# Waiting separately for the up and the down weights of the mixed slots, and a constant distance of three slots for the row requests

## The reference

```python
x = x + _L0_attn_ref(_layernorm(x, axis=-1), ...)     # delta-rule attention, 8 heads
x = x + _L0_ffn_ref(_layernorm(x, axis=-1), ...)      # mixture of experts
```

```python
cw = _combine_weights(xt, gate_w)          # four of 16 experts for each token
for e in range(E):
    a = _swiglu(xt @ expert_up_w[e].T)     # silu(gate half) * up half, 352 wide each
    out = out + cw[:, e:e + 1] * (a @ expert_down_w[e].T)
out = out + _swiglu(xt @ shared_up_w.T) @ shared_down_w.T
```

## Time and profile before

| what | value |
|---|---|
| median of three runs | 1292.75 us |
| profiled execution, its own time | 1290.94 us |
| its span, first to last instruction | 1289.1 us |
| PE busy | 1227.8 us, 95% of the span |
| DVE busy | 844.3 us, 65% |
| ACT busy | 367.2 us, 28% |
| POOL busy | 339.4 us, 26% |
| mean granted clock of TensorE | 0.977 |

### The profile page before, as it was taken

One profiled execution on the slowest core, in us unless ns is written; L12 is line 12 of the kernel. 1 busy time (PEld: TensorE's weight loads), 2 busy tenths in 40 slices (PEclk: granted clock), 3 DMA queues, 4 the chain that ended last, 5 costly groups with the idle time before them and its releaser, 6 DMA issues. The chain is left out here.

```text
span 1289.1 us, 26529 instructions
## 1 busy us (share of the span) xinstructions
PE 1227.8 (95%) x8747; PEld 750.4 (58%) x8747; DVE 844.3 (65%) x2352; ACT 367.2 (28%) x808; POOL 339.4 (26%) x401
## 2 busy tenths in 40 slices
PE   7979999999999999999999989999999999998985
PEld 6857778877776555444444544555555555554543
DVE  4897698768769475244511475777777777775763
ACT  4755655654453323220000011111111111111111
POOL 1302324322333122114653021222221122122212
PEclk9989999998997999999999998999999999998998
DMA  5434853742653494275457784878787878787642
GB/s 166 92 52 86 146 122 82 163 126 62 133 123 125 123 240 106 89 242 195 178 185 252 215 200 109 226 177 224 171 225 186 213 175 214 182 220 186 151 93 25
DMA packets 214306, 202.42 MB, mean 157 GB/s; under 512 B 72608, under 2 KB 154528, under 8 KB 214176
## 3 DMA queue, kind: packets, MB, share of 16 engines
q1 hardware_dynamic: 130080, 112.25, 33.3%
q10 hardware_dynamic: 67456, 54.24, 16.2%
q0 software_dynamic: 16640, 34.24, 12.2%
HBM read 123.76 MB, written 81.08 MB: 159 GB/s over the span
## 5 line engine op out<-in xcount | busy, mean ns | idle before, releaser
L2321 DVE STREAM_TRANSPOSE ups<-a 32x96 f32<-32x96 f32 (+1 forms) x1136 | 296.9, 261 | 35.4
L2191 POOL DMA_INDIRECT out<-front_region,ix x64 | 99.7, 1558 | 375.7 <-DMA out<-front_region,ix 148.5
L2446 PE MATMUL pD<-w,ups 128*128 (+1 forms) x384 | 176.7, 596 | 1.0 <-DVE ups L2321 0.7
L2433 PE MATMUL pG<-w,xsT 128*128 x512 | 162.9, 461 | 0.4 <-ACT g L2260 0.3
L2433 PE MATMUL pU<-w,xsT 128*128 x512 | 161.9, 459 | 0.0
L981 PE MATMUL pProj<-front_region 128*128 128x256 f32 x624 | 155.7, 393 | 2.2 <-ACT front_region L716 1.6
L2433 PEld LDWEIGHTS pG<-w,xsT 128*128 128x128 f32 x512 | 96.1, 189 | 75.2 <-issue 34.1
L2433 PEld LDWEIGHTS pU<-w,xsT 128*128 128x128 f32 x512 | 97.3, 190 | 54.2
L981 PEld LDWEIGHTS pProj<-front_region 128*128 128x128 f32 x624 | 113.8, 192 | 20.4 <-ACT front_region L716 2.1
L2260 ACT ACTIVATE g<-pG 128x352 f32<-128x352 f32 x72 | 33.4, 464 | 314.5 <-issue 121.6
L2446 PEld LDWEIGHTS pD<-w,ups 128*128 128x128 f32 (+1 forms) x384 | 71.9, 190 | 79.8 <-issue 69.2
(11 more groups left out here) (312 smaller groups left out, 1795.7 us busy)
## 6 DMA issues: line engine op xcount, KB each, us to landing
w<-in_expert_T SPq DMA_DIRECT2D x80, 384.0 KB
front_region<-in_expert_T ACTq DMA_DIRECT2D x64, 352.0 KB, 4.3
slot_rows<-zeros SPq DMA_DIRECT2D x72, 266.0 KB
front_region<-slot_rows ACTq DMA_DIRECT2D x288, 64.0 KB, 3.8
front_region<-in_expert_T ACTq DMA_DIRECT2D x32, 256.0 KB, 3.5
front_region<-in_L_attn_hidden_states SPq DMA_DIRECT2D x16, 256.0 KB, 4.0
x2r<-in_L_attn_hidden_states SPq DMA_DIRECT2D x16, 256.0 KB, 4.1
partial_sums<-x2r SPq DMA_DIRECT2D x16, 256.0 KB, 3.1
```

The lines of the kernel that those rows point to most:

```text
L2191: pool.indirect_dma_start(out=flat, out_offset=bass.IndirectOffsetOnAxis(ap=to[:, 0:1], axis=0), in_=y[(q - 1) % RING][:, :], in_offset=No ...
L2321: dve.transpose(aT[par][B * to:B * to + B, 0:n, rows], a[rows, 0:len(IC) * P].rearrange("p (c n) -> p c n", c=len(IC))[:, 0:n, B * to:B * ...
L2433: mm = pe.matmul(out[:, 0:I], rows[:, k, :], w[:, bass.ds(weights[0], 1), 2 * I * k + at:2 * I * k + at + I], start=(k == 0), stop=(k == D ...
L2446: return pe.matmul(out[:, :], gated_[0:m, c, :], w[0:m, bass.ds(weights[0], 1), at:at + D], start=(c == 0), stop=(c == 2))
```

## The change

Two independent edits, both in the slot stage.

1. The 14 pieces of a mixed slot now count on two semaphores: the eight of up weights on `s_wm`, the six of down weights on `s_wmd`. The gate product of a mixed slot waits for the up weights only. A new wait for the down weights stands ahead of the down product of the mixed slot, which is in the next body.
2. The helper `rows_by` is gone. Body 0 asks for rows 0 to 3, and body q from 1 on asks for rows q+3. Requests for routing data stay two slots ahead. The wait inside `load_rows` is the same expression, so it now looks for a transpose one slot earlier.

```diff
-                for r in range(max(2, rows_by(q - 1)), rows_by(q)):
-                    load_rows(r)
+                    load_rows(2)
+                if q + RING - 1 < NQ:
+                    load_rows(q + RING - 1)
...
-                    act.dma_start(wm[0:n, h, at:at + width], rows[0:n, at:at + width]).then_inc(s_wm, 16)
+                    act.dma_start(wm[0:n, h, at:at + width], rows[0:n, at:at + width]).then_inc(s_wm if c < DC else s_wmd, 16)
...
-                        pe.wait_ge(s_wm, 32 * (DC + len(IC)) * (before_mixed(q) + 1))
+                        pe.wait_ge(s_wm, 32 * DC * (before_mixed(q) + 1))
...
+                    if is_mixed(q - 1):
+                        pe.wait_ge(s_wmd, 32 * len(IC) * (before_mixed(q - 1) + 1))
```

More of the change, by code:

```diff
@@ L2091, in experts @@
     s_pos, s_read, s_routed = sem("pos_ready"), sem("counts_read"), sem("routed")
-    s_wm, s_out = sem("mixed_weights_loaded"), sem("mixed_rows_out")
+    s_wm, s_wmd, s_out = sem("mixed_up_loaded"), sem("mixed_down_loaded"), sem("mixed_rows_out")
     route_act, route_pool, route_pe, route_dve, list_dve = routing(nc, es, pD[0], w[:, 2], lg, xall, pos, lists,
@@ L2223, in load_meta @@
                 act.dma_start(mt[q % RING][:, :], mv[block_of(q)][:, D:RW]).then_inc(s_ml[q % RING], 16)
-            def rows_by(q):
-                return min(NQ, q + 1 + AHEAD + min(q, RING - AHEAD))
             def part_of(q):
```

## The result

In the first comparison the changed kernel takes 1271.05 us (median of four runs, 1268.95 to 1280.29), the kernel before 1292.66 us. The ratio is 0.984, with a 95% interval of 0.981 to 0.987. Two later sets have less of a gain: 1276.71 us against 1292.02 (ratio 0.988, 0.984 to 0.992) and 1276.22 against 1294.63 (0.988, 0.984 to 0.991). The sixteen runs of the changed kernel together have a median of 1275.0 us and reach from 1268.95 to 1284.84. So the change is worth 15 to 22 us between medians. Its runs spread somewhat more than those of the kernel before: standard deviation 5.1 us over the sixteen, against 3.7 us over 44 runs of the kernel before (1288.75 to 1302.06). The second difference is the less certain one.

The account below looks back on a forecast made before the run. PE was taken to bound the slot stage. 1290.94 - 22.65 - 1.03 + 0.7 = 1267.96 us from the profiled execution, 1269.8 from the median; predicted 1269 us, range 1264 to 1275, or to 1277 with most of POOL's rival.

Parts of the forecast that it names:

- What the three slots wait for: Gate products of mixed slots 7, 60 and 68 wait for down-weight pieces they do not read; gaps together 17.00 us.
- 22.65 us for the split: Excess of slots 7, 60 and 68 over slot 16's 7.56 us, all to go with the split wait.
- 1.03 for the rows: Loss between gate products 2 and 4, to go because body 2 asks for one row set less; 1.03 us.
- The clock's part: Behind the three gaps, gate products run partly at 1.2 GHz instead of 2.4; 5.65 us, to go with the standstills.
- The new wait costs nothing: Down-weight wait ahead of a mixed slot's down product: weights land with 6 us to spare, cost nothing.
- nor do rows asked later: Later bodies: rows asked three slots ahead have 14.4 us before their transpose, slowest landing 6.3 us; cost nothing.
- The tail, 0.7 us: End of kernel: POOL's additions, without the pause at slot 60, finish later; 0.7 us added, between nothing and 5.8.
- The lag at slot 59: Sign to look for: POOL's addition for slot 59 starts about 7 us behind ACT's copy for it.
- Rival 1: POOL becomes the end, not following PE's earlier finish; 5.1 us on top of the forecast, 1274 us; chance 0.13.
- the forecast (1269): Whole kernel: both edits bring their gains less a small tail, 1269 us; chance 0.80.
- the ring: Ring of four rows, about 22 us: POOL's lag was said to be always worked off before reaching it.
- the upper bound of the tail: End of kernel: POOL's lag after slots 58 to 70 at 6.15 us per addition; 5.8 us, judged too high.

Follow-up runs that it names:

- e4: Kernel before with five extra matmuls ahead of the unchanged weight wait of slots 7, 60 and 68; ratio 0.996 to the kernel before, median 1287.8 us.
- e1: Kernel before with only the split wait, row requests still four slots ahead; median 1274.1 us, ratio 0.986 to the kernel before.
- e6: Changed kernel with rows asked for two slots ahead instead of three; median 1274.95 us against 1276.71 for the changed kernel in the same set.
- e5: The changed kernel run again, unaltered, in a second set; median 1276.7 us, ratio 0.988 to the kernel before.
- e12: The changed kernel run a third time, unaltered; median 1276.2 us, ratio 0.988 to the kernel before.
- e7: Changed kernel with three row buffers and rings of five for the products, their scales and indices; median 1276.15 us.
- e8: Changed kernel with three row buffers, product rings of five, and two mixed slots one slot sooner (51 and 59); median 1273.74 us.
- e10: Changed kernel with SyncE's expert weights from the fourth expert on cut to 16 columns a piece; median 1268.96 us.
- e9: Changed kernel with the two additions of a mixed slot taking 64 rows each instead of 128; median 1266.83 us, ratio 0.979 to the kernel before.
- e3: Changed kernel without POOL's second addition at the eight mixed slots; median 1267.15 us.
- e11: Changed kernel with 64-row additions at mixed slots, and mixed slots at 51 and 59 instead of 52 and 60; median 1269.85 us.

## Why the prediction held, and where it did not

- **What the three slots wait for.** Right. With only the up weights in the wait the gaps are gone, 2.67 us from down product to gate product.
- **22.65 us for the split, 1.03 for the rows.** The middle part fell by 24.58 us; the 0.90 us more than the sum are hitches of 0.17, 0.23 and 0.50 us at slots 33, 39 and 40 in the profile of before, of unknown cause, that came back in neither profile of the changed kernel with a low lag. The clock's part is confirmed by e4. The 1.03 us are one profile's number: the same place cost 2.1 us in e1.
- **The new wait costs nothing, nor do rows asked later.** Right, and e6 shows that even two slots of distance would do, if only just: the slowest rows, 6.3 us in the profile of before, took 8.1 in the one after, and in e6 DVE waited for them twice. The Trainium skill's rule to issue early and wait late ("DMA: Bandwidth & Descriptors", "Rules for kernel authors") was set against this edit. Here it makes no measurable difference whether rows are asked for three or two slots ahead (1276.7 and 1274.95 us).
- **The tail, 0.7 us.** This term was mis-sized. It is 2.72 us in the first profile, 6.20 in e5 and 6.13 in e12 (37.08 and 37.01 us after gate product 70, against 30.88). I had bounded it by 5.8, which e5 and e12 pass, and gone to the lower end, on the argument that transfers thin out at the end. That argument held: from slot 61 to 70 the first profile has 5.61 us per addition, where I had 5.78. The lag at slot 59 came out as said, 7.09 us. What failed are the three intervals that end at the two additions of slot 60 and the one of slot 61: 8.71, 6.46 and 6.85 us, 22.0 together where the sum had 3 x 6.15 = 18.45. The lag rose to 14.14 us and 3.40 were left at slot 70, not 0.7.
- **Rival 1 against the forecast.** By the first four runs the forecast (1269) is nearer to the 1271.05 us, by all sixteen (1275.0) the rival (1274) is. It was rated at 0.13, too low. Its text also lacked half of the mechanism: I wrote that the lag was always worked off before the ring bit. In e1, e6, e7, e8 and e12 it was not, and POOL's lag went through `take_meta` on DVE into PE.
- What let me go wrong: the profile before shows lags of 6 to 13 us between slots 35 and 58, and POOL at 26% busy. I priced one execution's lag at one place. The comparison that mattered was 6.6 to 6.8 us for each serial addition while POOL lags, against a PE that, gaps removed, hands over one per 6.59 us. I had taken 6.15 from a single interval. Of the three pauses of PE the one at slot 60 was what kept POOL level: there the lag fell from 7.94 us at slot 58 to 0.78 at slot 59. Ahead of slots 7 and 68 it stood at 0.78 already.
- The prediction set the Trainium skill's figure for HBM access, 0.2 us on average and 2 us at high load ("DMA: Bandwidth & Descriptors", "Latency and other measured facts"), beside the upper bound of the tail. That bound, 5.8 us from rows, was nearer to e5 and e12 than my 0.7. e10 agrees with the direction of the figure: less traffic, landings 0.4 us shorter, no backlog at the end. That it is latency in HBM no run here shows.

Open: what decides in a given execution whether the lag stays at 10 us or passes 20. The same kernel did both.

## What to carry to other kernels

When a pause of the bounding engine is removed, ask which serial chain had been catching up in it, and compare rates over the whole stage: the chain's time per item, its completion wait included, against the new time per item of the engine that feeds it. Busy share does not show such a chain (POOL was at 27% when it set the end). A wait on a count of loads should cover only those that the next instruction reads. If a chain has no margin in its rate, make its items cheaper (e9) or fewer (e3); the deeper ring of e7 and e8 did not help.

## What the runs showed of the hardware

- An indirect addition of 64 rows instead of 128 with half of them out of bounds saved 0.14 us of POOL's 1.56 us, and 0.5 to 1.3 us of the landing: medians of 4.7 us in e9 and e11, 5.2 to 6.0 in the eight profiles with 16 such additions of 128 rows and no pause of PE at mixed slots. (With the pauses the medians were 5.1, 5.1 and 4.5 us.) So rows sent out of bounds are not free.
- After standstills of 6.21, 6.20 and 4.41 us the matmuls ran at 1.2 GHz for part of the next product (granted clock 0.50 over its first 2 us at slots 60 and 68, and from 776 to 780 us at slot 7); five dummy matmuls (4.46 us) inside the wait kept them at 2.4 GHz (2.42 us from gate to up product at slot 7), worth 6.1 us between medians for three waits.
- Shorter standstills went both ways: after 2.18 us (e12) the granted clock fell to 0.50, which cost some 1.5 us (1.79 behind gate product 58 against 0.26 in e1), after 2.29, 2.33 and 2.35 us (e1, e8, e7) it stayed at 1.00.
